# Hybrid layer, 8 batches on one core: the feed-forward residual enters the down product through VectorE, and the first and last batch are done in two parts

## The chip, the cores and the metric

The kernel runs on one core of one Trainium2 chip. Its time is the device time of one execution in microseconds (us); the median of several executions is compared.

## The reference, cut to what is computed

Each of 8 batches is a block `x` of 512 tokens x 128 channels in float32 and goes through five stages. `ln` is the plain normalization over channels with eps 1e-5.

```python
x = x + attention(ln(x))            # linear attention: ln(x) @ (Gram matrix of ln(x) @ Wq), no softmax
x = x + ffn(x)                      # f1
x = x + time_mix(ln(x))             # a recurrence over tokens with decay (maxima, exponentials), gate sigmoid(r), Wo
x = x + channel_mix(ln(x))          # square(relu(k)) @ Wv, gate sigmoid(r)
x = x + ffn(x)                      # f2

def ffn(x):
    y = ln(x)
    z = y + relu(y @ W1 + b1) @ W2 + b2      # 128 -> 512 -> 128
    return ln(z) * gamma + beta
```

The 16 feed-forwards (`f1` and `f2` of 8 batches) have the same weights. What matters here is the line of `z`: before its normalization, the down product needs `y + b2` added. Subtracting from each row of `z` its own mean changes nothing in `ln(z)`, so both kernels centre `W2` and `b2` over the channels.

## The kernel before, in words

A batch lies in SBUF as 128 partitions x 4 row blocks x 128 channels (`P` = 128, `J` = 4), in its own buffer `R[b]`, into which every stage adds. PSUM has 8 banks of 128 x 512; a call names its bank by number. Nothing schedules at run time: each engine has its order written out by hand as one long list of calls, such as `hidden_up(6, f2, 0, 2)` (batch, feed-forward, quarter, bank), and semaphores inside the calls make it wait. So the engine runs its list strictly in order, and a call that waits holds everything behind it. Batches overlap because the lists interleave calls of several batches.

One feed-forward `f` of batch `b` goes like this:

- VectorE `ffn_stats` and `mean_var` (L422, L460): statistics of `x`. GpSimd works out the scale (`shift`, `power`, `bias`), ScalarE writes `y` (`ffn_normed`, L758) into the ring `f1_y` or `f2_y`, which has 4 tiles.
- TensorE `ffn_transpose` (L993): 4 transposes of `y` into a bank. ScalarE `ffn_evacuate` (L813) copies them to `f_yT` and adds the centred `b2` (`B2C`) as bias.
- TensorE `hidden_up` (L1032): four products 128x512; each is evacuated by ScalarE `relu` (L821) into `f_h` with bias `B1C`. `B1C` is `b1` less what `B2C` brings into the up product, which TensorE `bias_part` (L1132) and VectorE `up_bias` work out at the start. The ring of `f_h` has 2 tiles.
- TensorE `ffn_start` (L1039): 4 transposes of `f_yT` against the identity, which put `y + b2` back into token order in the bank of the down product. This is done for 12 of the 16 feed-forwards. TensorE `ffn_down` (L1048): 4 quarters x 4 row blocks accumulate onto it.
- For the other 4 (`f2` of batches 1, 3, 5, 6, the table `IN_SBUF`) the down product starts at zero. GpSimd issues a DMA `down_residual` (L348) that adds `B2R` to `f_y` in SBUF, and VectorE `z_sum` (L449) adds the bank to it.
- VectorE `z_stats` (L422) or `z_sum_stats`, `mean_var`; GpSimd `z_shift` and `power` (L306, L311); VectorE `ffn_scaled` (L497) or `z_sum_scaled` (L508): 4 operations of 128x128; GpSimd issues the DMA `ffn_sum` that adds the result to `R[b]`. For `f1` of batch 0 and `f2` of batch 7 (`SPLIT`) VectorE does it itself instead: `ffn_gain` (L475) and `ffn_out` (L483).

The time mix has on VectorE the two recurrences `running_max` (L539) and `denominator_sum`/`numerator_sum`, and ends for each batch with VectorE `gated` (L598), TensorE `product_o` (L1078) and VectorE `tmix_out` (L606). The channel mix of that batch can start only then: its norm, TensorE `cmix_up` (L1090), `cmix_down` (L1096) and `gate_product` (L1107), then the norm and products of `f2`.

At the start the SP queue carries all loads, batches 0 and 1 first, and all weights. TensorE runs 24 transposes of the identity as warm-up, one small bias product, and 20 more transposes (`warm_up`, L1113) before the first Gram product (`attn_gram`, L1005). VectorE makes the normalized tile of batch 0 (`attn_normed`, L658) as a whole; `attn_out` (L466) adds attention to `R[b]`. `decay_along_tokens` clears `WROW` (L688) before it fills it. At the end the batch 7 result is made and stored as a whole.

The lines that carry this:

```python
IN_SBUF = {"f2": (1, 3, 5, 6)}
# ffn_start, TensorE
t_.matmul(banks[bank][:, j * C:(j + 1) * C], at(f.yT, b)[:, j * P:(j + 1) * P], IDENT[:], start=(j == 0), stop=False,
          is_transpose=True, skip_group_check=True)
# z_sum, VectorE
v.tensor_tensor(at(f.y, b)[:], bank_rows(bank), at(f.y, b)[:], ALU.add).then_inc(f.z_ready, 1)
```

## Time and profile before

| | us |
|---|---|
| median of 3 runs | 265.48 (265.29 to 265.97) |
| profiled execution | 266.14 |
| its span | 264.3 |
| granted TensorE clock, mean over the span | 0.992 |
| TensorE busy | 255.3 (97%) |
| VectorE busy | 228.2 (86%) |
| ScalarE busy | 227.2 (86%) |
| GpSimd busy | 159.0 (60%) |

The span runs from the first to the last instruction of the profiled execution; the 1.8 us that its time is longer lie around it. Busy time of an engine counts its records, and neighbouring records of one engine overlap a little, since an instruction is recorded until its last write while the next one is already in the pipeline. So the step from one start to the next tells what an operation costs in a row of them.

### The profile page before, as it was taken

What the parts mean: (1) busy time and instruction counts of PE and PEld (TensorE: products, weight loads), DVE (VectorE), ACT (ScalarE), POOL (GpSimd) and SP (SyncE); (2) the same over time, 40 slices, a digit from 0 to 9 for tenths busy, and PEclk for the clock granted to TensorE, in tenths of its full rate; (3) what the DMA queues carried; (4) which work ended last, traced back from release to release, by engine and by line L of the source; (5) the groups of instructions that cost most, each with busy time, mean ns of one, the idle gap of its engine ahead of it and who ended that gap; (6) DMA issues with size and microseconds to landing.
All of it is one profiled execution on the core that took longest, in us unless ns stands there. A gap on an engine that the chain in (4) does not pass through costs nothing. (4 is left out here: it accounts for less than half of the span.)

```text
span 264.3 us, 5318 instructions
## 1 busy us (share of the span) xinstructions
PE 255.3 (97%) x1544; PEld 191.7 (73%) x1544; DVE 228.2 (86%) x748; ACT 227.2 (86%) x440; POOL 159.0 (60%) x298
## 2 busy tenths in 40 slices
PE   7999999999999999999999999999999999999990
PEld 7987886866876686776588658757778658678770
DVE  3498569999999999999999999999999998637443
ACT  1397988999999999999989999999989979895630
POOL 4457676482498179179659827956069637445641
PEclk9999999999999999999999999999999999999996
DMA  6930420203022226303704130622046744725574
GB/s 184 297 110 0 82 42 1 42 15 64 2 42 40 40 42 103 58 2 67 133 2 75 18 67 2 119 41 43 0 71 120 126 85 115 126 43 87 118 150 122
DMA packets 18316, 19.15 MB, mean 72 GB/s; under 512 B 1520, under 2 KB 11632, under 8 KB 18288
## 3 DMA queue, kind: packets, MB, share of 16 engines
q0 software_dynamic: 7056, 12.85, 28.4%
q1 hardware_dynamic: 11232, 5.97, 8.0%
q8 instruction: 12, 0.20, 0.3%
q14 instruction: 16, 0.13, 0.2%
HBM read 3.87 MB, written 2.10 MB: 23 GB/s over the span
## 5 line engine op out<-in xcount | busy, mean ns | idle before, releaser
L1048 PEld LDWEIGHTS bank<-W,f_h 128*128 128x128 f32 x512 | 61.9, 192 | 8.4 <-issue 6.7
L1048 PE MATMUL bank<-W,f_h 128*128 128x128 f32 x512 | 64.3, 275 | 0.0
L1032 PE MATMUL bank<-f_yT,W 128*128 128x512 f32 x128 | 62.3, 598 | 0.0
L821 ACT ACTIVATE f_h<-bank,B1C 128x512 f32<-128x512 f32 x64 | 41.6, 681 | 9.5 <-PE bank L1032 8.2
L1096 PEld LDWEIGHTS bank<-FWv,KK 128*128 128x128 f32 x256 | 31.7, 192 | 5.0 <-issue 3.6
L1096 PE MATMUL bank<-FWv,KK 128*128 128x128 f32 x256 | 33.6, 275 | 0.0
L1032 PEld LDWEIGHTS bank<-f_yT,W 128*128 128x128 f32 x128 | 21.1, 190 | 16.7 <-issue 7.7
L1090 PE MATMUL bank<-XK,FWk 128*128 128x512 f32 x64 | 30.7, 599 | 0.0
L758 ACT ACTIVATE f_y<-R,f_yn_nb,f_yn_rs 128x128 f32<-128x128 f32 x64 | 26.3, 488 | 0.2 <-POOL f_yn_nb L315 0.2
L878 ACT ACTIVATE KK<-bank 128x512 f32<-128x512 f32 x32 | 18.4, 592 | 2.4 <-PE bank L1090 2.3
L882 ACT ACTIVATE KK<-KK 128x512 f32<-128x512 f32 x32 | 19.5, 625 | 0.1
L311 POOL TENSOR_TENSOR f_zn_rs<-f_zn_ve,K_RSQRT 128x4 f32<-128x4 f32 x16 | 18.9, 1183 | 0.5
L311 POOL TENSOR_TENSOR f_yn_rs<-f_yn_ve,K_RSQRT 128x4 f32<-128x4 f32 x16 | 18.6, 1161 | 0.0
L1090 PEld LDWEIGHTS bank<-XK,FWk 128*128 128x128 f32 x64 | 10.9, 190 | 9.8 <-issue 5.3
L339 POOL DMA_DIRECT2D R<-BETA x16 | 15.0, 964 | 4.6 <-ACT f_y L758 3.1
L293 POOL TENSOR_TENSOR tmix_tmp<-tmix_mv,K_EPS 128x4 f32<-128x4 f32 x8 | 2.5, 310 | 25.4 <-DVE tmix_mv L460 25.4
L306 POOL TENSOR_TENSOR f_zn_ve<-f_zn_mv,K_EPS 128x4 f32<-128x4 f32 x16 | 7.5, 469 | 16.6 <-DVE f_zn_mv L460 16.6
L364 POOL DMA_DIRECT2D R<-G x7 | 7.4, 1050 | 14.7 <-DVE G L634 14.7
L422 DVE BATCH_NORM_STATS2 f_yn_stats<-R 128x6 f32<-128x128 f32 x64 | 13.8, 278 | 2.0 <-DMA R<-G 1.7
L758 ACT ACTIVATE N<-R,tmix_nb,tmix_rs 128x128 f32<-128x128 f32 x32 | 13.1, 482 | 0.9 <-POOL tmix_nb L315 0.9
L758 ACT ACTIVATE NC<-N,cmix_nb,cmix_rs 128x128 f32<-128x128 f32 x32 | 13.1, 483 | 0.0
L284 POOL TENSOR_TENSOR f_yn_ve<-f_yn_mv,K_EPS 128x4 f32<-128x4 f32 x16 | 4.3, 270 | 14.5 <-DVE f_yn_mv L460 14.4
(144 smaller groups left out, 655.2 us busy)
## 6 DMA issues: line engine op xcount, KB each, us to landing
R<-BETA POOLq DMA_DIRECT2D x16, 256.0 KB, 3.4
R<-f_zg POOLq DMA_DIRECT2D x10, 256.0 KB, 3.4
R<-in_hidden SPq DMA_DIRECT2D x8, 256.0 KB, 3.9
R<-N POOLq DMA_DIRECT2D x8, 256.0 KB, 3.6
out_x<-R SPq DMA_DIRECT2D x8, 256.0 KB, 2.3
R<-G POOLq DMA_DIRECT2D x7, 256.0 KB, 3.5
f_y<-B2R POOLq DMA_DIRECT2D x4, 256.0 KB, 5.7
R<-f_y POOLq DMA_DIRECT2D x4, 256.0 KB, 3.9
```

The source lines that it names most:

```text
L306: pool.tensor_tensor(n.ve[b % 2][:], n.mv[b % 2][:, :, 1], K_EPS[:], ALU.add).then_inc(n.scale.sem(b), 1)
L311: pool.tensor_tensor(n.rs[b % 2][:], n.ve[b % 2][:], K_RSQRT[:], ALU.pow).then_inc(n.scale.sem(b), 1)
L339: pool.dma_start(R[b][:], BETA[:], accum_op=ALU.add).then_inc(*f.xb.step(b))
L422: last = v.bn_stats(n.stats[b % 2][:, j, :], src[:, j, :])
L758: done = a.activation(dst[:, j, :], src[:, j, :], ACT.Identity, scale=n.rs[b % 2][:, j:j + 1], bias=n.nb[b % 2][:, j:j + 1])
L821: a.activation(at(f.h, b)[:, n, :], banks[bank][:], ACT.Relu, bias=B1C[:, n:n + 1]).then_inc(f.h_ready[n], 1)
L878: a.activation(at(KK, b)[:, n, :], banks[bank][:], ACT.Relu).then_inc(square[n].sem(b), 1)
L882: a.activation(at(KK, b)[:, n, :], at(KK, b)[:, n, :], ACT.Square).then_inc(square[n].sem(b), 1)
L1032: t_.matmul(banks[bank][:], W1[:, n * P:(n + 1) * P], at(f.yT, b)[:], start=True, stop=True).then_inc(f.h_psum[n], 1)
L1048: last = t_.matmul(banks[bank][:, j * C:(j + 1) * C], at(f.h, b)[:, n, j * P:(j + 1) * P], W2[:, n, :], start=(n == 0 and j == 0 and b in ...
L1090: t_.matmul(banks[bank][:], FWk[:, n * P:(n + 1) * P], at(XK2, b)[:], start=True, stop=True).then_inc(kk_psum[n], 1)
L1096: last = t_.matmul(banks[bank][:, j * C:(j + 1) * C], at(KK, b)[:, n, j * P:(j + 1) * P], FWv[:, n, :], start=(n == 0 and j == 0), stop=(n ...
```

## The change

1. `ffn_start` moves from TensorE to VectorE. For all 16 feed-forwards VectorE writes `f_y + B2R` into the bank before the down products, with one `tensor_tensor` 128x512 (15 times), and for the last feed-forward with two, 128x384 and 128x128 (`last_start`). `ffn_down` always accumulates (`start=False`) and waits for that write (`f.y_psum`). The 48 transposes at L1039, `down_residual`, `z_sum`, `z_sum_stats` and `z_sum_scaled` are gone.
2. `ffn_evacuate` is a plain copy, `relu` takes `B1` as it is, and `bias_part` and `up_bias` are gone. `B2R` is one 128x128 tile, made by TensorE `bias_rows` (2 products) and VectorE `bias_rows_centred` (4 small operations).
3. The rings of `f_y` have 3 tiles instead of 4, those of `f_h` 1 instead of 2. `ffn_normed` waits for the VectorE write too before it overwrites a tile.
4. Batch 0: its load is two DMAs of 128 KB, and statistics, scale and `XN` are made in two halves of two row blocks (`first_stats`, `first_mean_var`, `first_shift`, `first_power`, `first_normed`).
5. Batch 7, `f2`: bias write, last down products, statistics, scale, gain, output and store are made in two parts, row blocks 0 to 2 and row block 3.
6. Loads: SP takes the 8 batches first, then the weights of the two mixes. The seven others (vectors, `Wq`, `W1`, `b1`, `W2`, `gamma`, `beta`) are issued by ScalarE's queue.
7. Warm-up: 10 float32 products of a zeroed tile, started as soon as VectorE has cleared it, and none after the bias products.
8. The lists of calls of all four engines are written anew, and with them the bank numbers.

The core of the diff:

```diff
-COPIES = {"N": 3, "f1_y": 4, "f2_y": 4, "f1_yT": 2, "f2_yT": 2, "f1_h": 2, "f2_h": 2, "XN": 3, "XNT": 2, "GRAM": 2,
-          "PROJ": 2, "f1_zg": 3, "f2_zg": 3, "others": 1}
+COPIES = {"N": 3, "f1_y": 3, "f2_y": 3, "f1_yT": 2, "f2_yT": 2, "XN": 3, "XNT": 2, "GRAM": 2, "PROJ": 2,
+          "f1_zg": 3, "f2_zg": 3, "others": 1}
-IN_SBUF = {"f2": (1, 3, 5, 6)}
+STARTED = {"f1": tuple(range(BATCHES)), "f2": tuple(range(BATCHES))}
+FIRST, LAST = ((0, 1), (2, 3)), ((0, 1, 2), (3,))
...
+            def ffn_start(b, f, bank, *free):
+
+                if b == f.started[0]:
+                    dve.wait_ge(*b2_rows.done(0, "centred"))
+                for s, count in free:
+                    dve.wait_ge(s, count)
+                dve.wait_ge(*f.norm.ready.done(b, "all"))
+                v.tensor_tensor(bank_rows(bank), at(f.y, b)[:], B2R[:].unsqueeze(1).broadcast_to([P, J, C]), ALU.add).then_inc(f.y_psum, 1)
...
             def ffn_down(b, f, n, bank, *free):
                 if b == 0:
-                    pe.wait_ge(w2_centred, 1)
-                freed(free)
+                    pe.wait_ge(*w2_rows.done(0, "centred"))
+                if b in f.started:
+                    pe.wait_ge(f.y_psum, f.started.index(b) + 1)
                 pe.wait_ge(f.h_ready[n], b + 1)
...
-                a.activation(at(f.yT, b)[:], banks[bank][:], ACT.Identity, bias=B2C[:]).then_inc(f.yT_ready, 1)
+                if b in f.started:
+                    a.activation(at(f.yT, b)[:], banks[bank][:], ACT.Copy).then_inc(f.yT_ready, 1)
...
+            def warm_up(bank, count):
+
+                pe.wait_ge(*warm.done(0, "tile"))
+                for _ in range(count):
+                    last = t_.matmul(banks[bank][:, 0:P], WROW[:, 0:P], WROW[:, 0:P], start=True, stop=True)
+                last.then_inc(warm.sem(0), 1)
```

How the lists move, at three places. A row is a line, an operation with its tiles, a shape and how many there are in a row.

**TensorE from the last `product_o` (batch 7) on.** Before, the first twelve rows from it (`L1048` is `ffn_down`, `L1032` `hidden_up`, `L1096` `cmix_down`, `L1090` `cmix_up`):

```order
L1078 MATMUL bank<-Wo,G 128x128 x4
L993 MATMUL bank<-IDENT,f_y 128x128 x4
L1048 MATMUL bank<-W,f_h 128x128 x8
L1032 MATMUL bank<-f_yT,W 128x512
L1096 MATMUL bank<-FWv,KK 128x128 x4
L1032 MATMUL bank<-f_yT,W 128x512
L1096 MATMUL bank<-FWv,KK 128x128 x4
L993 MATMUL bank<-IDENT,NC 128x128 x4
L1032 MATMUL bank<-f_yT,W 128x512
L1096 MATMUL bank<-FWv,KK 128x128 x4
L1032 MATMUL bank<-f_yT,W 128x512
L1090 MATMUL bank<-XK,FWk 128x512 x3
```

Now (`L1119` is `ffn_down`, `L1110` `hidden_up`, `L1187` `cmix_down`, `L1181` `cmix_up`, `L1198` `gate_product`):

```order
L1168 MATMUL bank<-Wo,G 128x128 x4
L1110 MATMUL bank<-f_yT,W 128x512 x3
L1187 MATMUL bank<-FWv,KK 128x128 x12
L1119 MATMUL bank<-W,f_h 128x128 x4
L1069 MATMUL bank<-IDENT,NC 128x128 x4
L1119 MATMUL bank<-W,f_h 128x128 x4
L1187 MATMUL bank<-FWv,KK 128x128 x4
L1119 MATMUL bank<-W,f_h 128x128 x4
L1181 MATMUL bank<-XK,FWk 128x512 x4
L1069 MATMUL bank<-IDENT,f_y 128x128 x4
L1119 MATMUL bank<-W,f_h 128x128 x4
L1198 MATMUL bank<-FWr,DC 128x128 x4
```

Three `hidden_up` products and the down products of channel mix 6 now stand together behind the last `product_o`, and down products of `f2` 4 and all those of `f2` 5 to 7. From the last `product_o` to the end of the list there were 16 products 128x512, 92 of 128x128 and 20 transposes; now there are 19, 104 and 16.

**VectorE before the first `running_max`.** Before (`L475` is `ffn_gain`, `L483` `ffn_out`, both of `f1` 0):

```order
L475 TENSOR_TENSOR f_zg<-bank,GAMMA 128x512
L422 BN_STATS f_zn_stats<-bank 128x6 x4
L422 BN_STATS attn_stats<-R 128x6 x4
L460 BN_AGGR f_zn_mv<-f_zn_stats 128x2 x4
L483 SCALAR_TENSOR_TENSOR R<-f_zg,f_zn_rs,R 128x128 x4
L422 BN_STATS tmix_stats<-R 128x6 x4
L460 BN_AGGR tmix_mv<-tmix_stats 128x2 x4
L466 TENSOR_TENSOR R<-bank,R 128x512
L422 BN_STATS f_yn_stats<-R 128x6 x4
L688 MEMSET WROW 128x512
L690 TENSOR_SCALAR WROW<-WROW,WDEC 128x512
```

Now (`L540`, `L548` are the same two, `L702` is `ffn_start`):

```order
L702 TENSOR_TENSOR bank<-f_y,B2R 128x512
L442 BN_STATS f_zn_stats<-bank 128x6 x4
L525 BN_AGGR f_zn_mv<-f_zn_stats 128x2 x4
L540 TENSOR_TENSOR f_zg<-bank,GAMMA 128x512
L702 TENSOR_TENSOR bank<-f_y,B2R 128x512
L548 SCALAR_TENSOR_TENSOR R<-f_zg,f_zn_rs,R 128x128 x4
L525 BN_AGGR attn_mv<-attn_stats 128x2 x4
L442 BN_STATS tmix_stats<-R 128x6 x4
L525 BN_AGGR tmix_mv<-tmix_stats 128x2 x4
L531 TENSOR_TENSOR R<-bank,R 128x512
L753 TENSOR_SCALAR WROW<-WROW,WDEC 128x512
```

`ffn_start` of `f1` 1 and 2 stand in front of and between the work on batch 0; the clearing of `WROW` is gone from here (it is the first call of the list). In all, 3 `ffn_start` stand ahead of the first `running_max`, and one `attn_out` and one `ffn_stats` with its `mean_var` fewer than before.

**VectorE around the last `gated` (`G<-EA,G`).** Before:

```order
L594 SCALAR_TENSOR_TENSOR G<-bank,G 128x512
L625 SCALAR_TENSOR_TENSOR DC<-DC,VEC,XC 128x512
L449 TENSOR_TENSOR f_y<-bank,f_y 128x512
L598 TENSOR_TENSOR G<-EA,G 128x512
L422 BN_STATS f_zn_stats<-f_y 128x6 x4
L460 BN_AGGR f_zn_mv<-f_zn_stats 128x2 x4
L606 SCALAR_TENSOR_TENSOR N<-N,tmix_back,bank 128x128 x4
L422 BN_STATS cmix_stats<-N 128x6 x4
L460 BN_AGGR cmix_mv<-cmix_stats 128x2 x4
L629 SCALAR_TENSOR_TENSOR G<-bank,G 128x512
L422 BN_STATS f_zn_stats<-bank 128x6 x4
```

Now:

```order
L688 TENSOR_TENSOR G<-bank,G 128x512
L648 SCALAR_TENSOR_TENSOR G<-bank,G 128x512
L652 TENSOR_TENSOR G<-EA,G 128x512
L442 BN_STATS f_zn_stats<-bank 128x6 x4
L660 SCALAR_TENSOR_TENSOR N<-N,tmix_back,bank 128x128 x4
L442 BN_STATS cmix_stats<-N 128x6 x4
L525 BN_AGGR cmix_mv<-cmix_stats 128x2 x4
L562 SCALAR_TENSOR_TENSOR f_zg<-bank,f_zn_rs,GAMMA 128x128 x4
L702 TENSOR_TENSOR bank<-f_y,B2R 128x512
L442 BN_STATS f_yn_stats<-R 128x6 x4
L525 BN_AGGR f_zn_mv<-f_zn_stats 128x2 x4
```

`z_sum` (`L449`) and its statistics are gone, and `ffn_start` of `f2` 4 stands behind `gated`. Between the first `running_max` and the last `gated` the list has now 9 `ffn_start` and one `attn_out` more, 2 `z_sum` and one scaling (4 operations of 128x128) fewer; nothing else changes in number there.

## Rows read from the trace of the kernel before

**Rows 1.** The page, first section: busy time, share of the span and instructions of each engine.
```profile
PE 255.3 (97%) x1544; PEld 191.7 (73%) x1544; DVE 228.2 (86%) x748; ACT 227.2 (86%) x440; POOL 159.0 (60%) x298
```

**Rows 2.** Busy time by stretch: us, busy (x) of PE, PEld, DVE, ACT, POOL; PEclk, DMA, GB/s.
```profile
9.50:45.60 36.10, 35.71 (x247) 28.96 (x246) 25.75 (x135) 30.79 (x77) 22.71 (x52) 1.00 0.32 75
45.60:220.10 174.50, 174.40 (x1019) 125.92 (x1017) 173.51 (x485) 168.73 (x313) 110.21 (x187) 1.00 0.31 55
220.10:257.60 37.50, 37.19 (x238) 28.82 (x237) 20.86 (x88) 26.43 (x51) 19.74 (x32) 1.00 0.56 104
```

**Rows 3.** Timeline of TensorE: start us, us, engine, line, operation, count.
```profile
253.55 3.73 PE L1048 MATMUL bank<-W,f_h 128*128 128x128 f32 x32
...
103.65 1.88 PE L1090 MATMUL bank<-XK,FWk 128*128 128x512 f32 x4
...
108.32 0.60 PE L993 MATMUL bank<-IDENT,f_y 128*128 128x128 f32 x4
```

**Rows 4.** Groups by line and shape: count | busy us, mean ns of one | idle before.
```profile
L1039 PE MATMUL bank<-IDENT,f_yT 128*128 128x128 f32 x48 | 7.2, 273 | 0.0
...
L449 DVE TENSOR_TENSOR f_y<-bank,f_y 128x512 f32<-128x512 f32 x4 | 2.7, 671 | 3.8 <-PE bank L1048 3.8
...
L688 DVE MEMSET WROW<- 128x512 f32 x1 | 0.5, 485 | 0.1
```

**Rows 5.** Timeline of VectorE: first `running_max`, last `gated`, last `tmix_out`.
```profile
45.57 1.22 DVE L539 TENSOR_TENSOR_SCAN PP<-WROW,bank 128x512 f32<-128x512 f32 x1
...
219.38 0.68 DVE L598 TENSOR_TENSOR G<-EA,G 128x512 f32<-128x512 f32 x1
...
221.38 1.12 DVE L606 SCALAR_TENSOR_TENSOR N<-N,tmix_back,bank 128x128 f32<-128x128 f32 x4
```

**Rows 6.** Timeline of TensorE, last `product_o`.
```profile
220.21 1.13 PE L1078 MATMUL bank<-Wo,G 128*128 128x128 f32 x8
```

**Rows 7.** Timeline of VectorE, two stretches of work back to back.
```profile
100.17 0.68 DVE L634 TENSOR_TENSOR G<-bank,G 128x512 f32<-128x512 f32 x1
100.77 0.68 DVE L614 TENSOR_TENSOR DC<-XC 128x512 f32<-128x512 f32 x1
...
203.44 1.13 DVE L508 SCALAR_TENSOR_TENSOR f_y<-f_y,f_zn_rs,GAMMA 128x128 f32<-128x128 f32 x4
204.49 0.86 DVE L422 BATCH_NORM_STATS2 cmix_stats<-N 128x6 f32<-128x128 f32 x4
```

**Rows 8.** Timeline of VectorE, the start.
```profile
3.54 0.87 DVE L422 BATCH_NORM_STATS2 attn_stats<-R 128x6 f32<-128x128 f32 x4 [3.54 <-DMA R<-in_hidden]
...
6.43 1.11 DVE L658 TENSOR_SCALAR XN<-R,attn_mv,attn_rs 128x128 f32<-128x128 f32 x4 [0.43 <-POOL attn_rs L311]
...
13.30 0.69 DVE L466 TENSOR_TENSOR R<-bank,R 128x512 f32<-128x512 f32 x1 [3.33 <-PE bank L1020]
...
33.98 1.14 DVE L483 SCALAR_TENSOR_TENSOR R<-f_zg,f_zn_rs,R 128x128 f32<-128x128 f32 x4 [1.42 <-POOL f_zn_rs L311]
```

**Rows 9.** Timeline of TensorE, the start: warm-up, first Gram product, last down products of `f1`, batch 0.
```profile
1.53 5.38 PE L1113 MATMUL bank<-IDENT 128*128 128x128 f32 x24 [1.53 <-POOL IDENT L264]
...
7.00 2.67 PE L1113 MATMUL bank<-IDENT 128*128 128x128 f32 x20
...
9.50 1.06 PE L1005 MATMUL bank<-XN 128*128 128x128 f32 x8
...
27.96 1.95 PE L1048 MATMUL bank<-W,f_h 128*128 128x128 f32 x16
```

**Rows 10.** Timelines of VectorE and GpSimd, the end.
```profile
257.32 0.89 DVE L422 BATCH_NORM_STATS2 f_zn_stats<-bank 128x6 f32<-128x128 f32 x4 [2.78 <-PE bank L1048]
...
258.98 1.03 POOL L311 TENSOR_TENSOR f_zn_rs<-f_zn_ve,K_RSQRT 128x4 f32<-128x4 f32 x1
...
260.05 1.14 DVE L483 SCALAR_TENSOR_TENSOR R<-f_zg,f_zn_rs,R 128x128 f32<-128x128 f32 x4 [0.85 <-POOL f_zn_rs L311]
```

**Rows 11.** The page, last section: line engine op xcount, KB, us to landing.
```profile
out_x<-R SPq DMA_DIRECT2D x8, 256.0 KB, 2.3
```

798 lines of the change are left out of this document (424 added, 374 removed).

## The prediction, made before the changed kernel was run

> **What bounds the kernel now.** I read the page's busy shares first [rows 1]: TensorE is 97% busy and VectorE 86%. Such a mean hides stages, so next comes the busy time by stretch [rows 2], cut at the first `running_max`, at the last `gated` and at TensorE's last product [rows 5]. The reader is to see three regimes. In 45.6 to 220.1 TensorE has records over all of it, but VectorE too: 173.51 of 174.50 us. A matmul's record includes waiting in a full pipeline, so I count TensorE's work instead. The steps are 0.427 us for a pass of 512 columns ((1.88 - 0.6) / 3), 0.1115 us for one of 128 ((3.73 - 0.275) / 31), 0.108 us for a transpose ((0.60 - 0.275) / 3) [rows 3]; a float32 product has two passes. By these the whole list is 242.4 us before. From the last `product_o`, at 220.21 [rows 6], the listed 32 long passes (13.7), 184 short ones (20.5) and 20 transposes (2.2) are 36.4 us, and the trace takes 37.1 up to TensorE's end at 257.3. So the last stretch is bounded by TensorE, which works off what it has left over, while VectorE is busy 20.86 of 37.5 us there. The middle is bounded by VectorE: its list between the two landmarks is 175.9 us by such steps, and the trace took 174.5. In the first stretch VectorE is busy 25.75 of 36.1 us: it waits there in turn for TensorE, GpSimd and DMAs [rows 8, 9]. So there are four terms: start of the middle, its length on VectorE, the rest on TensorE, and the end.
>
> My landmarks are the start of the first `running_max` (45.57), the last `gated`, the last product, and the end of the span (264.3).
>
> **The start: -5.3 us.** Batch 0's statistics begin at 3.54, when 256 KB have landed; TensorE's first Gram product is held until 9.50 by the second warm-up block, 2.67 us from 7.00, although `XN` is there from 7.5 on [rows 8, 9]. Now the first half needs 128 KB, and no warm-up stands behind the bias products. I walked the new lists with the old durations. First statistics at 3.1 (estimate: 0.4 less for half the load), `XN` whole at 6.9, `attn_out(0)` at 10.85 instead of 13.30, so 2.45 less. The first up product comes at 17.8. The last down product of `f1` 0 ended at 29.9 (27.96 + 1.95) and ends at 25.8: the four start transposes and two products that stood in front are gone. From there `ffn_out(0)`, time-mix norm, transposes, `mix_k` and `product_k` follow as before. Had they kept their distance, `running_max(0)` would come 4.1 us earlier; VectorE's list ahead of it has 3 starts more (+1.8) and one `attn_out` and one norm pass less (-1.7), so it is about 30 us either way and doesn't hold it. Some of the 16 us of idle time that remain are filled by the new order. I take 40.3, thus -5.3. Ends: -3.5 (only the changes at batch 0, with a wait at the moved loads) and -12 (VectorE never idle after 3.1: 3.1 + 30.2 = 33.3).
>
> The new warm-up is a question of its own. The first 24 transposes took 5.38 us, twice the step of the later 20, although the profile shows a granted clock of 1.00 there [rows 9]. If the products from 7 us on ran at that double step, some 3 us of it would be on the path; this is in the low end of the -3.5.
>
> **The middle, VectorE: +3.7 us.** Between `running_max(0)` and `gated(7)` come in 9 `ffn_start` and one `attn_out`; 2 `z_sum` go, and one scaling of four 128x128. A start is a `tensor_tensor` 128x512 from SBUF into PSUM with a broadcast operand. No row before has it. The nearest rows are adds that read a bank, step 100.77 - 100.17 = 0.60 us [rows 7], with a record of 671 ns [rows 4]; the lowest is the clearing of 128x512 at 485 ns [rows 4], the highest the four 128x128 at 1.05 [rows 7]. I take 0.60, nearest in shape and operands; the ends 0.45 and 0.75 make +-1.4. So 9 x 0.60 + 0.60 - 2 x 0.60 - 1.05 = +3.75. In this stretch every start counts in full, since VectorE is idle for under 1 us of it. The time TensorE saves here is not on the path: 9 of the 12 x 4 transposes it loses, and only 146 to 164 us of listed work in 158 to 178 us. ScalarE's list between its gate calls is 158 us before and 159 after. It saves 16 x 0.09 us on the copies without bias, and isn't the one that is late. I cost both at nothing. `down_residual` goes from GpSimd, four issues of some 2 us each, on an engine that is 60% busy [rows 1]: nothing. The shorter rings cost nothing either: `ffn_normed(b)` needs the reading of `y` of batch b-3, and `relu` of b the downs of b-1, which stand ahead of its up products at nearly all places. If that cover fails, the price is in the slower case below.
>
> **After the last `product_o`, TensorE: +4.8 us.** The order excerpt shows what moved. Behind it stand now 38 long passes (16.2), 208 short (23.2) and 16 transposes (1.7), together 41.2 us against 36.4. The 48 transposes at L1039 are 5.2 us of TensorE's list [rows 3, 4], yet only four of them stood here. The new order has TensorE idle in the middle and leaves it 19 products instead of 16 for the end. VectorE isn't in the way there: 20.86 us before plus some 5 in 41. Ends: +3 (part of these products is done while `tmix_out(7)` and its norm would leave TensorE waiting anyway; but the row shows only 0.7 us of such waits now) and +6.
>
> By the Trainium skill, "Perfetto Trace Analysis", Identifying the Most-Contended Engine, matmul busy time is no good measure for TensorE, and the busy share of weight loads is to be read in its place. That is 73% over the span [rows 1] and 28.82 of 37.5 us, 77%, in this stretch [rows 2]. By that rule TensorE isn't the bound here, and this term would fall away; the sum by rows says 36.4 of 37.1.
>
> **The end: -0.9 us.** From the last product to the end are 7.06 us: statistics at 257.32, power 1.03 us at 258.98, `ffn_out` 260.05 to 261.19 [rows 10], then the store, 256 KB in 2.3 us from issue to landing [rows 11]. Now three quarters of it start two products (0.45 us) before the last. Powers follow each other on GpSimd, so the second ends at about +2.9 and the last `ffn_out` at +3.5 instead of +3.9; 64 KB land sooner, by 0.5 as an estimate (nothing to 1.1). Ends: -0.3 and -1.6.
>
> **Sum.** -5.3 + 3.7 + 4.8 - 0.9 = +2.3 us. The profiled execution takes 266.14 with a span of 264.3, so it would be 268.4. It stands 0.66 above the median of 265.48, so the median is forecast at **267.8**. A difference of 0.3% (0.8 us) is what a measurement of this kernel can tell from none.
>
> **The rivals.**
>
> *A, faster: the start gains more.* 16 us of idle time stand in VectorE's first stretch, and the new lists put starts, statistics and the later batches' attention between the waits. If `running_max(0)` comes at 35.3, 5 us sooner than in my walk and 2 above the floor, the time is 262.8. For: the order was changed most here, and seven loads left the SP queue. Against: the chain of `f1` 0 (transposes, up, relu, down, norm, power) is no shorter by its own links.
>
> *B, the skill's rule.* TensorE isn't the bound of the last stretch, and the added products fill gaps: 267.8 - 4.8 = 263.0. Against: the 36.4 of 37.1 above.
>
> *C, the same.* A start gain of 7.5 us: -7.5 + 3.7 + 4.8 - 0.9 = +0.1, 265.5.
>
> *D, slower: a start holds VectorE.* `ffn_start` waits in VectorE's strict order for ScalarE's `y` and, in 9 calls, for a bank to be read by another engine. Behind it stand the operations of the recurrence, which nothing else feeds. With the forecast otherwise, 12 such starts at 0.3 us each put on 3.3 to 3.6 us: 271. It decides from 0.1 us per start on. For: the old lists had no such wait, and VectorE has no slack. Against: they were placed where the bank should have been free.
>
> That the change doesn't do what it says is out: the list has no transposes against `f_yT` any more, and 15 + 2 writes on VectorE.
>
> **How the numbers follow.** Forecast 0.42 (267.8), A 0.28 (262.8), C 0.17 (265.5), D 0.10 (271), B 0.03 (263.0). Faster takes A and B, 0.31; same is C, 0.17; slower is the forecast and D, 0.52. The forecast's own range is 265.8 to 269.8. The range for 8 in 10 is 262.5 to 271.0: it takes in A's and D's middle and leaves out their far halves.
>
> **What would show it.** `running_max(0)` near 40.3; from there to the last `gated` about 178 us with VectorE idle for under 2; TensorE from the last `product_o` to its end about 41.9; from there to the end 6.2; `ffn_start` at 0.60 per step with no wait for banks. The prediction is wrong if `running_max(0)` is before 37, if TensorE's idle time in the middle is small so that the products of the end move forward, or if VectorE's starts show idle time ahead of them.

## The result, and the profile after

The changed kernel takes 272.94 us (median of 4, 270.95 to 273.63) against 265.73 us for the kernel before, run beside it. The ratio is 1.0252, 95% interval 1.0184 to 1.032: it is slower by 2.5%. The forecast was 267.8 us with a range up to 271.0. The direction was right, the size was not: +2.3 us were forecast, +7.2 us came.

The profiled execution of the changed kernel is its fastest, 270.95 us with a span of 269.2, 4.9 us above that of the kernel before. The other 2 us of the median are differences between executions; the traces of the experiments show two such differences. An execution over 1.5% longer than the fastest of its kernel counts in the medians and ranges below but in no ratio (one of a_res, the profiled one; two of a_chain; one of the kernel before, of 939 us).

The page's first section, then the busy time by stretch, cut at the same landmarks as in [rows 2] (columns as there):

```profile
PE 249.8 (93%) x1464; PEld 184.5 (69%) x1464; DVE 235.0 (87%) x764; ACT 227.3 (84%) x439; POOL 159.1 (59%) x296
```

```profile
42.30:220.80 178.50, 171.22 (x973) 121.45 (x971) 176.53 (x489) 167.96 (x312) 110.21 (x182) 1.00 0.27 46
220.80:262.40 41.60, 41.60 (x263) 32.12 (x262) 24.23 (x103) 29.94 (x58) 21.60 (x36) 1.00 0.56 105
262.40:269.20 6.80, 0.04 (x1) 0.00 (x0) 2.70 (x13) 0.00 (x0) 1.78 (x4) 0.77 0.68 158
```

In the middle VectorE is busy nearly all the time as before, while TensorE now has gaps: 171.22 of 178.50 us busy, where it had none in [rows 2]. Behind the last `product_o` TensorE has no gap in 41.6 us. The landmarks themselves, from the timelines of VectorE and TensorE (first `running_max`; last `gated`; last `product_o`; start of the last block of products; first statistics of the end), which answer to [rows 5, 6, 10]:

```profile
42.33 1.21 DVE L593 TENSOR_TENSOR_SCAN PP<-WROW,bank 128x512 f32<-128x512 f32 x1
...
220.00 0.69 DVE L652 TENSOR_TENSOR G<-EA,G 128x512 f32<-128x512 f32 x1 [0.70 <-ACT G L946]
```

```profile
220.88 1.09 PE L1168 MATMUL bank<-Wo,G 128*128 128x128 f32 x8
...
260.49 1.95 PE L1139 MATMUL bank<-W,f_h 128*128 128x128 f32 x16
```

```profile
262.03 0.69 DVE L447 BATCH_NORM_STATS2 f_zn_stats<-bank 128x6 f32<-128x128 f32 x3 [2.69 <-PE bank L1139]
```

The terms of the prediction, in us of the two profiled executions:

| term | before | after | measured | forecast |
|---|---|---|---|---|
| start of `running_max(0)` | 45.57 | 42.33 | -3.2 | -5.3 |
| from there to the start of the last `gated` | 173.8 | 177.7 | +3.9 | +3.7 |
| from there to the last `product_o` | 0.8 | 0.9 | 0 | 0 |
| from there to TensorE's end | 37.1 | 41.6 | +4.5 | +4.8 |
| from there to the end of the span | 7.0 | 6.8 | -0.3 | -0.9 |
| sum | 264.3 | 269.2 | +4.9 | +2.3 |

The two large losses have about the forecast size. The two gains are too small, and the timed executions lose more still. So I looked at the start first. VectorE's timeline:

```profile
3.16 0.49 DVE L447 BATCH_NORM_STATS2 attn_stats<-R 128x6 f32<-128x128 f32 x2 [1.76 <-DMA R<-in_hidden]
...
6.83 0.87 DVE L442 BATCH_NORM_STATS2 attn_stats<-R 128x6 f32<-128x128 f32 x4 [2.13 <-DMA R<-in_hidden]
7.62 0.58 DVE L467 TENSOR_SCALAR XN<-R,attn_mv,attn_rs 128x128 f32<-128x128 f32 x2
8.12 0.28 DVE L719 TENSOR_SCALAR DIAG<-IDENT,VEC 128x128 f32<-128x128 f32 x1
8.32 0.59 DVE L467 TENSOR_SCALAR XN<-R,attn_mv,attn_rs 128x128 f32<-128x128 f32 x2
...
13.80 0.69 DVE L531 TENSOR_TENSOR R<-bank,R 128x512 f32<-128x512 f32 x1 [0.32 <-PE bank L1097]
```

The first half of batch 0 is there at 3.16, as thought. But VectorE's list has the statistics of batch 1 ahead of `first_normed(0)`. They wait 2.13 us for their load, until 6.83, and XN(0), which needs nothing of batch 1, stands behind them. In the kernel before the statistics of batch 1 began at 4.75, behind those of batch 0, and XN(0) at 6.43 [rows 8]. TensorE in the same stretch, and the granted clock by windows (PEclk is the third column from the end, 1.00 is 2.4 GHz):

```profile
1.46 4.63 PE L1206 MATMUL bank<-WROW 128*128 128x128 f32 x20 [1.46 <-DVE WROW L713]
8.55 0.46 PE L1213 MATMUL bank<-DIAG,MEAN 128*128 128x128 f32 x2 [2.46 <-DVE DIAG L719]
...
8.98 1.14 PE L1082 MATMUL bank<-XN 128*128 128x128 f32 x8
9.96 1.01 PE L1069 MATMUL bank<-IDENT,XN 128*128 128x128 f32 x4
...
11.92 1.85 PE L1097 MATMUL bank<-PROJ,XNT 128*128 128x128 f32 x8 [0.52 <-ACT PROJ L873]
13.60 0.60 PE L1069 MATMUL bank<-IDENT,XN 128*128 128x128 f32 x4
```

```profile
9.00:10.00 1.00, 1.00 (x12) 1.00 (x11) 0.96 (x8) 0.00 (x0) 0.72 (x3) 1.00 1.08 328
10.00:11.00 1.00, 1.00 (x8) 1.00 (x5) 0.55 (x3) 0.28 (x1) 0.79 (x2) 0.51 1.20 301
11.00:12.00 1.00, 0.48 (x3) 0.22 (x2) 1.00 (x12) 0.99 (x3) 0.32 (x3) 0.50 1.22 290
12.00:14.00 2.00, 2.00 (x12) 2.00 (x13) 1.61 (x9) 2.00 (x6) 1.53 (x5) 0.64 1.16 297
```

The warm-up ends at 6.1, and TensorE has nothing to do for 2.46 us. It starts again with a step of 0.12 us in the first Gram product, and from 10 to 13 us it runs at the lower of its two levels, 0.50 of the clock: four transposes take 1.01 us where they take 0.60 later, eight passes of `attn_apply` 1.85 instead of 1.13. At the end, `last_out` waits 0.90 us for a DMA, R<-BETA:

```profile
264.96 1.14 DVE L493 SCALAR_TENSOR_TENSOR R<-f_zg,f_zn_rs,R 128x128 f32<-128x128 f32 x4 [0.90 <-DMA R<-BETA]
```

### The profile page after: what moved, and what is told of

It is laid out like the page before. It is cut to its first block and busy times, and to the rows that moved or that the text cites. A ratio compares the mean times of both kernels' runs of the same rounds, so it can differ in the third digit from the quotient of the medians.

```text
span 269.2 us, 5220 instructions
## 1 busy us (share of the span) xinstructions
PE 249.8 (93%) x1464; PEld 184.5 (69%) x1464; DVE 235.0 (87%) x764; ACT 227.3 (84%) x439; POOL 159.1 (59%) x296
## 5 line engine op out<-in xcount | busy, mean ns | idle before, releaser
L1119 PEld LDWEIGHTS bank<-W,f_h 128*128 128x128 f32 x480 | 58.1, 192 | 9.1 <-issue 9.1
L1110 PE MATMUL bank<-f_yT,W 128*128 128x512 f32 x128 | 62.1, 595 | 1.1 <-ACT f_yT L881 0.8
L1119 PE MATMUL bank<-W,f_h 128*128 128x128 f32 x480 | 61.3, 276 | 1.1 <-ACT f_h L895 0.9
L895 ACT ACTIVATE f_h<-bank,B 128x512 f32<-128x512 f32 x64 | 41.8, 685 | 8.3 <-PE bank L1110 5.7
L1187 PEld LDWEIGHTS bank<-FWv,KK 128*128 128x128 f32 x256 | 31.6, 192 | 7.7 <-issue 5.0
L1187 PE MATMUL bank<-FWv,KK 128*128 128x128 f32 x256 | 32.9, 276 | 0.0
L1110 PEld LDWEIGHTS bank<-f_yT,W 128*128 128x128 f32 x128 | 21.7, 191 | 15.5 <-issue 12.7
L1181 PE MATMUL bank<-XK,FWk 128*128 128x512 f32 x64 | 31.0, 597 | 0.5 <-ACT f_yT L881 0.3
L288 POOL TENSOR_TENSOR f_yn_ve<-f_yn_mv,K_EPS 128x4 f32<-128x4 f32 x16 | 7.3, 455 | 35.5 <-DVE f_yn_mv L525 35.4
L377 POOL DMA_DIRECT2D R<-f_zg x14 | 14.1, 1009 | 9.3 <-DVE f_zg L562 8.8
L1181 PEld LDWEIGHTS bank<-XK,FWk 128*128 128x128 f32 x64 | 11.0, 190 | 10.8 <-issue 7.5
L562 DVE SCALAR_TENSOR_TENSOR f_zg<-bank,f_zn_rs,GAMMA 128x128 f32<-128x128 f32 x56 | 15.6, 340 | 2.9 <-issue 2.9
L336 POOL TENSOR_TENSOR f_zn_ve<-f_zn_mv,K_EPS 128x4 f32<-128x4 f32 x15 | 5.6, 375 | 19.7 <-DVE f_zn_mv L525 19.6
L341 POOL TENSOR_TENSOR f_zn_rs<-f_zn_ve,K_RSQRT 128x4 f32<-128x4 f32 x15 | 16.2, 1080 | 0.9
L442 DVE BATCH_NORM_STATS2 f_zn_stats<-bank 128x6 f32<-128x128 f32 x60 | 13.2, 282 | 2.7 <-PE bank L1119 2.7
L702 DVE TENSOR_TENSOR bank<-f_y,B2R 128x512 f32<-128x512 f32 x15 | 10.3, 690 | 4.2 <-ACT f_y L828 4.1
```

Source lines behind the costliest of these rows:

```text
L341: pool.tensor_tensor(n.rs[b % 2][:], n.ve[b % 2][:], K_RSQRT[:], ALU.pow).then_inc(n.scale.sem(b), 1)
L377: pool.dma_start(R[b][:], at(tile, b)[:], accum_op=ALU.add).then_inc(*f.out.step(b))
L562: last = v.scalar_tensor_tensor(zg[:, j, :], z[:, j, :], f.znorm.rs[b % 2][:, j:j + 1], GAMMA[:], ALU.mult, ALU.mult)
L895: a.activation(at(f.h, b)[:, n, :], banks[bank][:], ACT.Relu, bias=bias[:, n:n + 1]).then_inc(f.h_ready[n], 1)
L1110: t_.matmul(banks[bank][:], W1[:, n * P:(n + 1) * P], at(f.yT, b)[:], start=True, stop=True).then_inc(f.h_psum[n], 1)
L1119: last = t_.matmul(banks[bank][:, j * C:(j + 1) * C], at(f.h, b)[:, n, j * P:(j + 1) * P], W2[:, n, :], start=False, stop=(n == H - 1), sk ...
```

## The experiments

All times are medians; "before" ran beside each group, with medians of 265.6 to 266.5 us and single executions from 264.7 to 267.6. The landmarks are those of each run's profiled execution: the first Gram product, the start of `running_max(0)`, the middle from there to the start of the last `gated`, the rest from the last `product_o` to TensorE's end. The edits are on the changed kernel, except the `b_` runs, which are on the kernel before.

| run | median (range) | Gram | running_max(0) | middle | rest |
|---|---|---|---|---|---|
| before | 265.5 | 9.50 | 45.57 | 173.8 | 37.1 |
| changed | 272.94 (270.95 to 273.63) | 8.98 | 42.33 | 177.7 | 41.6 |
| a_order | 273.31 (272.56 to 274.60) | 7.06 | 42.97 | 179.4 | 41.6 |
| a_warm | 272.67 (271.96 to 273.72) | 8.84 | 41.10 | 180.5 | 41.6 |
| a_oneq | 273.00 (272.36 to 273.37) | 6.83 | 41.45 | 180.5 | 41.6 |
| a_res | 275.29 (273.39 to 278.48) | 9.41 | 44.59 | 181.6 | 43.0 |
| a_warm_break | 270.60 (269.76 to 271.83) | 9.12 | 41.78 | 178.2 | 42.4 |
| a_start | 270.89 (270.17 to 271.18) | 7.45 | 40.78 | 178.4 | 41.6 |
| a_start_break | 270.01 (269.84 to 270.33) | 6.88 | 41.15 | 178.2 | 41.6 |
| a_nostart | 271.34 (270.62 to 272.00) | 8.86 | 44.15 | 176.6 | 41.5 |
| a_pestart | 274.37 (273.66 to 276.54) | 8.77 | 42.81 | 178.6 | 43.3 |
| sb_nostart | 267.95 (267.04 to 269.12) | 7.05 | 41.82 | 176.3 | 41.5 |
| sb_pestart | 272.01 (271.83 to 272.76) | 6.84 | 41.92 | 177.5 | 43.3 |
| a_lessdown | 271.88 (270.62 to 274.12) | 8.41 | 41.75 | 179.4 | 41.2 |
| a_chain | 275.63 (271.37 to 276.11) | 8.74 | 44.11 | 179.4 | 42.3 |
| a_chain_less | 271.61 (269.99 to 273.89) | 9.49 | 44.97 | 179.4 | 40.1 |
| b_dummy | 269.90 (269.66 to 270.48) | 8.56 | 45.10 | 177.8 | 37.1 |
| b_warm | 264.47 (264.27 to 264.68) | 7.79 | 43.95 | 173.8 | 37.1 |
| b_first | 264.30 (263.71 to 265.31) | 7.45 | 44.10 | 173.8 | 37.1 |
| b_best | 263.85 (263.76 to 264.52) | 6.47 | 43.22 | 173.8 | 37.1 |

### The start

**a_order.** XN(0) ahead of the statistics of batch 1.

```diff
-            first_normed(0); bias_diagonal(); first_normed(1); mean_var(1, na); attn_stats(2)
+            first_normed(0); bias_diagonal(); first_normed(1); attn_stats(1); mean_var(1, na); attn_stats(2)
```

(`attn_stats(1)` stood at the end of the line ahead of these.)

> Edit, on the changed kernel: VectorE makes XN of batch 0 (first_normed of both halves) before it takes the statistics of batch 1, not behind them. Theory 1 (VectorE's strict order: XN(0) stands behind the load of batch 1, so TensorE is idle from 6.09 to 8.55 us and then runs its next work at the low clock until 13): XN(0) is whole at about 6.7 instead of 8.9, the first Gram product comes at about 6.9 instead of 8.98, the recorded clock stays at 1.00, running_max(0) comes 2 to 3.5 us earlier than 42.33, and the kernel is 2 to 5 us faster than the changed one (272.94), 268 to 271. Rival (the later chain of the first feed-forward sets the start, not XN(0)): running_max(0) moves by less than 0.7 us, and the time stays within 1 us.

The first Gram product came at 7.06, as expected, but `running_max(0)` at 42.97 and the time at 273.31: no gain. TensorE's timeline of this run shows where the 1.9 us went:

```profile
9.66 1.13 PE L1097 MATMUL bank<-PROJ,XNT 128*128 128x128 f32 x8 [0.47 <-ACT PROJ L873]
13.22 0.66 PE L1069 MATMUL bank<-IDENT,XN 128*128 128x128 f32 x4 [2.43 <-DVE B2C L729]
13.71 1.59 PE L1082 MATMUL bank<-XN 128*128 128x128 f32 x8
15.10 1.06 PE L1069 MATMUL bank<-IDENT,XN 128*128 128x128 f32 x4
```

The transposes of batch 1 wait 2.43 us for B2C, since they go into bank 7, which holds the bias rows until B2C has been made from them. VectorE does that in `bias_rows_centred`, and this call stands in its list behind the statistics of batches 2, 3 and 4, which wait for their loads. After the pause TensorE soon runs at half rate again (1.06 us for four transposes; granted clock 0.50 from 15 to 17 us). The wait was already in the changed kernel's list, covered by the late XN(0).

**a_warm.** A longer warm-up.

```diff
-            warm_up(0, 10)
+            warm_up(0, 18)
```

> Edit, on the changed kernel: 18 warm-up products instead of 10, so that TensorE has no pause between 6.09 and 8.55 us. Nothing else changes. Theory of the clock (the fall to 0.5 of the clock from about 10 to 13 us follows the pause, and is worth over 1 us, more in the executions of 273.6 us): the clock stays at 1.00 there, the first Gram product is at most 0.5 us later, attn_out(0) comes at about 12.3 instead of 13.8, the median falls by 1 to 3 us and the executions of one kernel lie closer together than 270.95 to 273.63. Rival (the slow stretch is hidden behind GpSimd and ScalarE): no change beyond 0.7 us.

The clock stayed at 1.00, `attn_out(0)` came at 12.57 instead of 13.80 and `running_max(0)` at 41.10 instead of 42.33: the half clock was worth 1.2 us of the start in the profiled execution. Yet the time hardly moved (272.67). The middle had become 2.9 us longer, which is taken up below.

**a_oneq.** All loads on the SP queue, in the old order.

```diff
             load_x0(1)
+            sp.dma_start(Wq[:], w_q).then_inc(first_loaded, DMA)
+            sp.dma_start(VEC[:], vectors).then_inc(first_loaded, DMA)
             load_x0(2)
...
-            act.dma_start(VEC[:], vectors).then_inc(first_loaded, DMA)
-            act.dma_start(Wq[:], w_q).then_inc(first_loaded, DMA)
...
```

> Edit, on the changed kernel: all loads on the SP queue in the order of the kernel before, the first batch still in two halves; nothing is loaded by ScalarE's queue. Theory (two queues side by side share the 16 DMA engines, so batch 1, which XN(0) waits for in VectorE's order, lands at 6.8 us instead of about 5): its statistics start at about 5.0 to 5.4, XN(0) is whole 1.5 us earlier, the time falls by 1 to 3 us. Rival (batch 1 is late only by its place behind another load, or Wq and the vectors then come later on the one queue and hold the Gram and projection products): the start stays within 0.7 us or gets later.

Batch 1's statistics began at 4.67, the Gram product at 6.83; then the same kind of wait for B2C, 2.57 us, this time with no fall of the clock behind it, and the same longer middle as in a_warm: 273.00. So with the second queue batch 1 came 2 us later. `running_max(0)` came 0.9 us earlier than in the changed kernel, and the end gained nothing.

**a_start.** As a_order, and `bias_rows_centred` moved up, with 12 warm-up products.

```diff
-            mean_var(2, na); mean_var(3, na); attn_stats(4); bias_rows_centred(); attn_out(0, 0); ffn_stats(0, f1)
+            mean_var(2, na); mean_var(3, na); attn_stats(4); attn_out(0, 0); ffn_stats(0, f1)
...
+            first_normed(1); attn_stats(1); mean_var(1, na); bias_rows_centred(); attn_stats(2); attn_stats(3)
...
-            warm_up(0, 10)
+            warm_up(0, 12)
```

> Edit, on the changed kernel: on VectorE XN of batch 0 is made ahead of the statistics of batch 1, and bias_rows_centred ahead of the statistics of batch 2 (in the runs a_order and a_oneq TensorE stood idle for 2.4 us at attn_transpose(1), which waits for it, and bias_rows_centred stood behind the loads of batches 2 and 3); 12 warm-up products instead of 10. Theory (each gain at batch 0 was lost to the next VectorE call that stood behind a load, and TensorE's half clock followed each pause): the first Gram product at about 7.2, no pause of TensorE over 1 us before 18 us and no step of 0.21 us behind the warm-up, running_max(0) at 39.5 to 41, so 1.3 to 2.8 us before that of the changed kernel. Rival (something later in the start, the norm chain of f1 0 or its loads, holds): running_max(0) at 41.5 or later. What the time does depends on the middle: 269 to 272.

`running_max(0)` came at 40.78, where the prediction had 40.3, and the four executions lie within 1.01 us: 270.17 to 271.18. The walk of the prediction isn't confirmed by that, though: `attn_out(0)` came at 12.20, not 10.85, and the 1.35 us were made up for on the way to `running_max(0)`. The median fell by 2 us, though the middle (178.4) is no better than in the trace of the changed kernel. What timed executions of the changed kernel may have lost at the start can be seen in other runs that share it. In a_res, a_nostart, a_chain and a_chain_less `running_max(0)` came at 44.1 to 45.0, not 42.3. TensorE's timeline of a_res:

```profile
9.41 2.06 PE L1082 MATMUL bank<-XN 128*128 128x128 f32 x8
11.26 1.06 PE L1069 MATMUL bank<-IDENT,XN 128*128 128x128 f32 x4
...
13.27 2.04 PE L1097 MATMUL bank<-PROJ,XNT 128*128 128x128 f32 x8 [0.52 <-ACT PROJ L873]
...
15.96 1.78 PE L1082 MATMUL bank<-XN 128*128 128x128 f32 x8
17.58 0.60 PE L1069 MATMUL bank<-IDENT,XN 128*128 128x128 f32 x4
```

There the fast step (0.60 us for four transposes) comes only at 17.58; everything before it takes twice as long, although the windows give a granted clock of 1.00 there (a_nostart and a_chain read the same; a_chain_less reads 0.50 from 9 to 18 us). With the same start in the lists, TensorE is at either level from one trace to the next. What it goes with is the pause: in all seven traces that share this start (the changed kernel, a_res, a_lessdown, a_nostart, a_pestart, a_chain, a_chain_less) 1.8 to 3.0 us pass between the 10 warm-up products and the next work, and each then runs at half rate for 3 to 9 us. In the eight other traces of the new order the pause is 1.5 us or less, and the first Gram product and its transposes run at the fast step.

### The middle

In a_warm and a_oneq the middle was 180.5 us instead of 177.7, with an edit that ended at 14 us. VectorE's idle time had grown around 127 us, in front of `gate_log(3)`, which waits for ScalarE, which waits for GpSimd's `bias(2, ncm)` (cmix_nb). GpSimd's timeline of a_warm, and VectorE's of the same microseconds:

```profile
119.67 1.03 POOL L341 TENSOR_TENSOR cmix_rs<-cmix_ve,K_RSQRT 128x4 f32<-128x4 f32 x1
120.78 1.78 POOL L345 TENSOR_TENSOR cmix_nb<-cmix_nm,cmix_rs 128x4 f32<-128x4 f32 x1
```

```profile
120.63 0.73 DVE L569 TENSOR_TENSOR DX<-XA 128x512 f32<-128x512 f32 x1
121.23 1.27 DVE L638 TENSOR_TENSOR EA<-AB,EA 128x1024 f32<-128x1024 f32 x1
...
127.11 0.69 DVE L648 SCALAR_TENSOR_TENSOR G<-bank,G 128x512 f32<-128x512 f32 x1 [1.11 <-ACT G L942]
```

An operation of 128x4, which takes 0.20 us elsewhere, took 1.78 us there, and 3.7 us in a_res (below). (a_res was profiled in its longest execution, 278.48 us.) While it waits VectorE runs operations with two tensors in SBUF, back to back. In a_warm it ends as the second of them does, in a_res as VectorE turns to statistics:

```profile
124.27 3.71 POOL L345 TENSOR_TENSOR cmix_nb<-cmix_nm,cmix_rs 128x4 f32<-128x4 f32 x1
```

```profile
124.11 0.74 DVE L569 TENSOR_TENSOR DX<-XA 128x512 f32<-128x512 f32 x1
124.71 1.28 DVE L638 TENSOR_TENSOR EA<-AB,EA 128x1024 f32<-128x1024 f32 x1
125.84 0.81 DVE L581 SCALAR_TENSOR_TENSOR XV<-DX,VEC,XA 128x512 f32<-128x512 f32 x1
126.51 0.75 DVE L644 SCALAR_TENSOR_TENSOR G<-G,EA 128x512 f32<-128x512 f32 x1
127.11 0.81 DVE L575 SCALAR_TENSOR_TENSOR XK<-DX,VEC,XA 128x512 f32<-128x512 f32 x1
127.77 0.95 DVE L442 BATCH_NORM_STATS2 f_zn_stats<-bank 128x6 f32<-128x128 f32 x4
```

The Trainium skill, "SBUF — State Buffer", Who interferes with whom, says that a VectorE instruction with two SBUF inputs and a GpSimd instruction that reads SBUF contend for a shared port, and that whoever issues first holds it for the whole instruction. The rows agree that the two keep each other out, but the wait outlasts one instruction: two of them in a_warm, five in a_res (124.27 to 127.98), where it ends with the first one that reads one tensor.

**a_warm_break.** One call moved, on top of a_warm, so that the run of such operations has a gap.

```diff
-            tmix_change(4); with_current(3); mix_v(4); gate_sum(3); mix_k(4); z_stats(6, f1, 6)
-            tmix_stats(5); gate_log(3, 1)
+            tmix_change(4); tmix_stats(5); with_current(3); mix_v(4); gate_sum(3); mix_k(4); z_stats(6, f1, 6)
+            gate_log(3, 1)
```

> Edit, on the run with 18 warm-up products: VectorE takes tmix_stats(5), four statistics with one tensor input each, between tmix_change(4) and with_current(3), where there was a run of five operations with two tensors in SBUF each; before, it stood behind that run. Theory P (in that run GpSimd's small operation bias(2, ncm) cannot start, 1.58 us with the longer warm-up and 3.5 us in the run with the earlier residual, and from it ScalarE's channel-mix norm, gate and VectorE's gate_log are late; that makes the middle 180.5 us instead of 177.7): bias(2, ncm) takes under 1.2 us, VectorE's idle time at gate_log(3) is under 0.7 instead of 1.11, the middle from running_max(0) to the last gated is 177.5 to 179.5, and the time falls by 1 to 3 us from 272.67. Rival (the middle's extra 2.9 us are elsewhere, the idle time at gate_log(3) is set by TensorE or the DMAs): the middle stays at 180 to 181.

`bias(2, ncm)` took 0.64 us, the idle time at `gate_log(3)` went, the middle fell from 180.5 to 178.2 and the time by 2.1 us to 270.60. So theory P holds for the wait, but not for the whole of the 2.9 us that it set out to explain. The time from `running_max(3)` to `running_max(5)` tells them apart:

| traces | `bias(2, ncm)` | from `running_max(3)` to `(5)` |
|---|---|---|
| changed | 0.20 | 46.7 |
| a_warm_break, a_start_break | 0.64 | 47.3 |
| a_order, a_start, a_lessdown, a_chain, a_chain_less | 1.78 | 48.4 to 48.5 |
| a_warm, a_oneq | 1.78 | 49.6 |
| a_res | 3.71 | 50.6 |

The wait of 1.78 us is worth 1.1 to 1.2 us against the broken run of operations and 1.7 us against the trace of the changed kernel. The further 1.1 us of a_warm and a_oneq go with TensorE's clock. In a_start and in a_warm alike TensorE stands idle for 1.65 us and 0.51 us around this place, since ScalarE is late; then the two passes of the product behind `mix_k` take 1.13 us in a_start and 1.70 in a_warm, where the window reads a clock of 0.50 (third column from the end; 0.53 in a_res from 130 to 132 us). In a_warm `running_max(4)` then waits 0.55 us for that product, in a_start not at all. Why the clock fell in one and not in the other isn't shown. The rows of a_start, of a_warm, and the window of a_warm:

```profile
125.32 1.13 PE L1152 MATMUL bank<-XK,Wk 128*128 128x512 f32 x2 [0.51 <-ACT f_h L895]
```

```profile
126.61 1.70 PE L1152 MATMUL bank<-XK,Wk 128*128 128x512 f32 x2 [0.51 <-ACT f_h L895]
```

```profile
128.00:130.00 2.00, 2.00 (x10) 1.90 (x9) 1.66 (x2) 2.00 (x5) 0.00 (x0) 0.50 0.04 12
```

Whether GpSimd's operation waits seems to hang on a tenth of a microsecond. In the trace of the changed kernel it starts 0.06 us before VectorE's `tmix_change` (DX), where it waits it starts 0.02 to 0.16 us behind it. Why it gets through after two operations in most traces and after five in a_res isn't shown. It waits in all ten other traces of the new order in which the run of operations isn't broken, so the changed kernel's profiled execution, its fastest, is the lucky one.

**a_start_break.** Both together.

> Edit: as a_start, and tmix_stats(5) between tmix_change(4) and with_current(3) as in a_warm_break. Theory (start and the locked-out GpSimd operation are separate and add up): running_max(0) as in a_start, bias(2, ncm) under 1 us, middle 177.5 to 178.5, time 267.5 to 269.5, near the forecast of 267.8. Rival (GpSimd's luck only moves to another of its operations): middle 179.5 or more.

270.01 us, 269.84 to 270.33: somewhat above what I expected. The middle was within it, `running_max(0)` came 0.4 us later than in a_start. This is the changed kernel without these accidents, and it is still 1.6% slower than before (1.0117 to 1.0202). Its terms are -4.4, +4.4, +4.5 and -0.3 us, +4.2 in all where +2.3 were forecast. Against a_start the break gave 0.9 us of the time.

**a_nostart, a_pestart; sb_nostart, sb_pestart.** The write of `y + b2` cut to one column (`[:, 0, 0:1]` of bank, `f_y` and `B2R`), without and with TensorE's transposes in its place; `sb_` on top of a_start_break. They leave `y + b2`, or `b2`, out of `z`.

```diff
-                v.tensor_tensor(bank_rows(bank), at(f.y, b)[:], B2R[:].unsqueeze(1).broadcast_to([P, J, C]), ALU.add).then_inc(f.y_psum, 1)
+                v.tensor_tensor(bank_rows(bank)[:, 0, 0:1], at(f.y, b)[:, 0, 0:1], B2R[:, 0:1], ALU.add).then_inc(f.y_psum, 1)
```

> Edit, on the changed kernel: each of the 17 writes of y + b2 is one column of 128x1 instead of 128x512, in the same place and with the same waits, and the down product starts at zero; y + b2 is left out of z. It takes 0.5 us each off VectorE and nothing off any other engine. Theory (VectorE bounds the middle, so each of its starts counts in full there; TensorE the rest): the 9 starts of the middle give 4 to 5 us, from 177.7 to about 173, the end from the last product_o stays at 41 to 41.6, and the time falls by 4 to 7 us to about 267.5 (with the three starts ahead of running_max(0)). Rival (GpSimd's and ScalarE's chains or TensorE bound the middle, and VectorE's added work is hidden): under 2 us.

> Edit, on the changed kernel: as the run with one column, and besides TensorE puts y into the bank by 4 transposes of f_yT ahead of the first down product, as the kernel before did, for all 16 feed-forwards; b2 is left out. So the new order of calls with the start on TensorE. 64 transposes are 6.9 us of TensorE work, 16 of them behind the last product_o. Theory (the middle is VectorE's, with room on TensorE; behind the last product_o all is TensorE's): middle about 1 us above the run with one column, the end from product_o 1.7 us longer, 43.3; in all 2 to 3 us slower than with one column, 269 to 271. Rival (TensorE is the bound of the middle too once it has the transposes back): middle 3 us or more above it, as slow as the changed kernel or slower.

The first pair was blurred by its starts (44.15 and 42.81). But the middle did not fall to 173 with 4.5 us of VectorE's work gone: 176.6, with 4.4 us idle. The clean pair:

> Edit: a_pestart on top of a_start_break, so without the bad start: the 17 writes of y + b2 are one column each, and TensorE puts y into the bank by 16 x 4 transposes; b2 is left out. This is the new order with its start mended and the start of the down product as in the kernel before. Theory (VectorE's 9 writes bound the middle, TensorE's transposes cost only in the rest): middle 174 to 177 instead of 178.2, rest 43.3 instead of 41.6, so the time within 1.5 us of a_start_break's 270.0, 268.5 to 271. Rival (TensorE bounds the middle as well once it has the transposes): middle over 178.5, time over 272.

> Edit: a_nostart on top of a_start_break: the new order with its start mended, the 17 writes of y + b2 one column each, no transposes; y + b2 is left out. Against a_start_break (270.0) it gives what the write costs on VectorE in the new order, against sb_pestart (272.0) what the transposes cost on TensorE. Theory (a stand-in of 0.6 us counted 0.57 us each in the old order, so VectorE's full price would be 4.5 us in the middle; but sb_pestart, with the 9 writes gone, had its middle only 0.75 us shorter, with 4.7 us of idle time on VectorE, so in the new order other waits take the write's place): middle 175.5 to 177, rest 41.5, time 267.5 to 269.5. Rival (sb_pestart's middle was held by the transposes, and without them the 4.5 us come off): middle under 174.5.

Against a_start_break (270.01) the 17 writes together are worth 2.1 us of the time (267.95), 1.9 of it in the middle. The transposes in their place are worth 4.1 (272.01); of that the profiled executions show 1.7 in the rest and 1.1 in the middle. So in the new order VectorE is the better place for the start. But even with no start at all the new order is slower than the kernel before (1.0077, 1.0045 to 1.0108), and that kernel has 12 starts and 4 sums in its time.

**b_dummy.** One more operation of 128x512 on VectorE ahead of each `tmix_change`, in the old order.

```diff
             def tmix_change(b):
+                v.tensor_tensor(SCRATCH[:], BETA[:], GAMMA[:].unsqueeze(1).broadcast_to([P, J, C]), ALU.add)
```

> Edit, on the kernel before: one more tensor_tensor of 128x512 on VectorE ahead of each tmix_change, that adds gamma to beta into a tile nobody reads; 7 of the 8 lie between running_max(0) and the last gated. Nothing waits for it and TensorE has the same work. Theory (VectorE bounds the middle, each 0.60 us operation counts in full): middle 173.8 + 4.2 = 178.0, time 269 to 270.5. Rival (half or more of it is hidden under waits of the other engines): middle under 176.

The middle went from 173.8 to 177.8: 4.0 us for 7 operations, 0.57 each. In the old order such an operation counts nearly in full. The time rose by 1.4% (1.0101 to 1.0176).

### Behind the last product_o, and the end

**a_lessdown.** Quarters 1 and 2 of the down products of `f2` 5 and 6 for one row block instead of four. The others are left out of the result.

```diff
-                for j in range(J):
+                for j in range(1 if f is f2 and b in (5, 6) and n in (1, 2) else J):
```

> Edit, on the changed kernel: in the second feed-forwards of batches 5 and 6 the quarters 1 and 2 of the down product are made for one row block instead of four; 12 products of 128x128 are left out, 24 passes of 0.1115 us or 2.7 us of TensorE, all behind the last product_o. Theory (TensorE's rest bounds the stretch of 41.6 us behind product_o): that stretch falls to 38.8 to 39.2, nothing ahead of it moves, and 2.5 us go from the time. Rival (it is bound by VectorE, ScalarE and GpSimd in turn, with TensorE's records only filled by waiting): it falls by under 1 us.

The rest fell by 0.4 us only, 41.6 to 41.2, with 2.7 us less of TensorE's work. By itself this says that TensorE doesn't bound it. The timeline shows another limit: the chain of batch 7 (TensorE now waits 0.73 us for ScalarE's last `f_y`). In the kernel before its last `cmix_down` began 20.1 us behind `product_o`, now 24.2 us, since four other calls stand ahead of it in TensorE's list:

```profile
241.09 1.05 PE L1187 MATMUL bank<-FWv,KK 128*128 128x128 f32 x8
241.98 1.95 PE L1119 MATMUL bank<-W,f_h 128*128 128x128 f32 x16
243.77 1.02 PE L1110 MATMUL bank<-f_yT,W 128*128 128x512 f32 x2
244.63 0.60 PE L1069 MATMUL bank<-IDENT,f_y 128*128 128x128 f32 x4
245.06 1.06 PE L1187 MATMUL bank<-FWv,KK 128*128 128x128 f32 x8
```

From there the chain goes on through `cmix_gated`, the norm of `f2` 7 and ScalarE's `f_y`, which ends 32.7 us behind `product_o`; TensorE comes to its transposes at 33.0. The two limits lie 0.3 us apart.

**a_chain, a_chain_less.** `cmix_down(7, 3)` right behind `cmix_down(7, 2)`, and the calls of ScalarE and VectorE that follow from it moved up (TensorE's list shown); then the same with the products left out.

```diff
-            hidden_up(5, f2, 1, 0, (f2.zg_ready, 5)); cmix_down(7, 2, 6); ffn_down(5, f2, 0, 7); ffn_down(5, f2, 1, 7)
-            hidden_up(5, f2, 2, 0); ffn_transpose(6, f2, 2); cmix_down(7, 3, 6); ffn_down(5, f2, 2, 7)
+            hidden_up(5, f2, 1, 0, (f2.zg_ready, 5)); cmix_down(7, 2, 6); cmix_down(7, 3, 6); ffn_down(5, f2, 0, 7); ffn_down(5, f2, 1, 7)
+            hidden_up(5, f2, 2, 0); ffn_transpose(6, f2, 2); ffn_down(5, f2, 2, 7)
```

> Edit, on the changed kernel, behind the last product_o: TensorE makes cmix_down(7, 3) right behind cmix_down(7, 2) and not 4 us later; ScalarE's cgate_back(7) stands ahead of ffn_normed(6) and ffn_normed(7) ahead of the relus of batch 6; VectorE's cmix_gated(7), cmix_out(7) and ffn_stats(7) ahead of ffn_start(6). So batch 7's y is ready some 3 us sooner; TensorE's work is the same. Two limits are held to lie within 0.5 us of each other there: TensorE's own 41.2 us of work, and the chain of batch 7 through channel mix and norm. If both are real: the stretch from product_o to TensorE's end stays at 41.0 to 41.6. If only the chain bounds it (rival, since 2.7 us less of TensorE's work gave 0.4): 38.5 to 40.

> Edit: a_chain and a_lessdown together (chain of batch 7 sooner, and 2.7 us of down products of batches 5 and 6 left out). If both limits are real: the stretch is now 38.5 to 39.2, over 2 us less than with either edit alone. If only the chain bounds it: as a_chain. If a third thing does (the last feed-forward's own ups, relus and downs behind a later wait): over 40.5.

With `f_y(7)` done 3.9 us sooner, at 28.8, the rest was 42.3, not shorter but 0.7 longer: TensorE stands idle for 0.48 us ahead of the last down products of `f2` 5. In a_chain_less, with the same wait, the profile puts it down to ScalarE's `f_h`, and the edit had put a call of ScalarE ahead of these `relu`. With the products left out as well it was 40.1, 2.2 us less than a_chain for 2.7 us of work; I had expected 38.5 to 39.2. Only with both edits does the rest fall clearly below the 41.6 of the changed kernel, by 1.5 us. So both limits are real, and they lie close together. (Both traces have the bad start, so their times say nothing.)

**a_res.** The last `ffn_residual` moved up in GpSimd's list.

```diff
-            z_shift(5, f2); power(5, f2.znorm)
+            ffn_residual(7, f2); z_shift(5, f2); power(5, f2.znorm)
...
-            ffn_sum(6, f2, f2.zg); ffn_residual(7, f2); last_shift(0)
+            ffn_sum(6, f2, f2.zg); last_shift(0)
```

> Edit, on the changed kernel: the last ffn_residual (DMA that adds beta to batch 7) is issued in GpSimd's list before the scale of batch 5's second feed-forward and not as the last DMA. Theory (the two-part end gained 0.3 us instead of 0.9 because last_out waits for that DMA, which is issued at 260.18 and lands at about 264.9): last_out starts at about 264.2 after last products at 262.4, and 0.7 us go from the end. Rival (the end is set by the second part's own power and store): nothing changes by over 0.3 us.

`last_out` no longer waited for the DMA and began 2.4 us behind `last_stats(0)` instead of 2.9, but from those statistics to the end of the span are 7.1 us as in the changed kernel (7.2), and 7.0 before. The rival holds: without the wait for the DMA the end is as long, with the second part's own power (0.55 us, until 272.69) and a store of 64 KB that lands in 1.9 us where 256 KB took 2.3 [rows 11]. The time itself, 275.29, goes with three losses in its trace. The half-step start and the locked-out operation are far from the edit. The third is the edit's own: the moved call waits 2.07 us for `f_y` of batch 7, and the scale of `f2` 5 now stands behind it in GpSimd's list; TensorE in the end waits 1.12 us for `ffn_scaled`, and the rest is 43.0.

### The start by itself, in the old order

**b_warm.** A shorter second warm-up block.

```diff
-            warm_up(0, 24); centre_bias(); warm_up(0, 20); attn_gram(0, 0)
+            warm_up(0, 24); centre_bias(); warm_up(0, 6); attn_gram(0, 0)
```

> Edit, on the kernel before: the second warm-up block has 6 transposes instead of 20. XN(0) is ready there at 7.5 us and the first Gram product stands behind the block at 9.50. Theory (the start carries through to the end, since the middle has no slack on VectorE): first Gram product at about 7.8, attn_out(0) 1.5 us earlier, running_max(0) 0.5 to 1.7 us earlier, time 264 to 265, the clock at 1.00. Rivals: the loads of batches 2 and 3 or the later chain hold and nothing moves (265.2 to 265.9); or the shorter block lets the clock fall and the time rises over 266.

**b_first.** Part 4 of the change put into the kernel before: two half loads, `first_stats` to `first_normed`, XN(0) ahead of `attn_stats(1)`, 4 transposes behind the bias product. Two groups of semaphores were merged to make room. One hunk of several:

```diff
-            attn_stats(0); mean_var(0, na); attn_stats(1); mean_var(1, na); attn_normed(0); centre_down_bias()
+            first_stats(0); first_mean_var(0); first_stats(1); first_mean_var(1); first_normed(0); first_normed(1); centre_down_bias(); attn_stats(1); mean_var(1, na)
```

> Edit, on the kernel before: part 4 of the change by itself, batch 0 loaded and normalized in two halves, with XN(0) ahead of the statistics of batch 1, and 4 transposes instead of 20 in the second warm-up block. Everything else, the starts on TensorE and all other calls in their places, is as before. Theory: XN(0) at about 6.3 and the first Gram product at about 7.3, running_max(0) at 43 to 44.5 instead of 45.57, middle, rest and end as before, time 263 to 264.8: a version faster than both. Rival (the gain at batch 0 is lost to the next call that waits for a load, as in a_order): running_max(0) within 0.5 us of before, time 265 to 266.

**b_best.** On b_first:

```diff
-            warm_up(0, 24); centre_bias(); warm_up(0, 4)
+            warm_up(0, 21); centre_bias(); warm_up(0, 3)
...
-            bias_part(); attn_apply(0, 0)
+            attn_apply(0, 0); bias_part()
```

> Edit, on b_first: 21 and 3 warm-up transposes instead of 24 and 4, and bias_part behind attn_apply(0) and not ahead of it (TensorE waited 0.44 us there for W1). Theory: the first Gram product at 6.7 to 7.0 instead of 7.45, attn_out(0) about 1 us earlier, running_max(0) at 43.3 to 43.8, time 263.2 to 264.0. Rival (the clock falls or rises later with less warm-up, or a later wait takes the gain): 264.3 or more.

264.47, 264.30 and 263.85: all three beat both kernels (intervals from 0.990 to 0.996), b_best by 0.6% of the kernel before (ratio 0.9939, 0.9916 to 0.9962). The gain at `running_max(0)` (1.6, 1.5, 2.4 us) arrives at the end nearly whole, with middle, rest and end unchanged. Up to 0.5 us of it is chance: b_dummy, whose start is untouched, has its `running_max(0)` at 45.10. The halves by themselves gave next to nothing over the shorter warm-up: in b_first XN(0) was whole at 6.4 and the Gram product was still held by the warm-up and the bias product until 7.45. For b_best a clean start came with it:

```profile
1.53 3.96 PE L1161 MATMUL bank<-IDENT 128*128 128x128 f32 x21 [1.53 <-POOL IDENT L271]
5.89 0.35 PE L1167 MATMUL bank<-VEC,MEAN 128*128 128x1 f32 x2 [0.41 <-DMA VEC<-in_vectors]
6.11 0.53 PE L1161 MATMUL bank<-IDENT 128*128 128x128 f32 x3
6.47 1.11 PE L1053 MATMUL bank<-XN 128*128 128x128 f32 x8
```

## Why the prediction was wrong

- **The start, -5.3 us, is the step that failed.** "`XN` whole at 6.9, `attn_out(0)` at 10.85": I walked the list with the old durations and took batch 1 to be there when its statistics were due. It landed at 6.8, XN(0) stood behind it in VectorE's list and was whole at 8.9, and `attn_out(0)` came at 13.80, no earlier than before. The excess over the forecast was 2.1 us in the profiled execution. With the order mended (a_start), `running_max(0)` came at 40.78, within 0.5 us of the walk; that is in part luck, since `attn_out(0)` was at 12.20 even then.
- **The warm-up.** I had priced the double step at up to 3 us of the low end and then taken none of it. It costs 1.2 us in the profiled execution (a_warm) and about 2 us more where the fast step comes only at 17 us. The traces with this loss are those with a pause of 1.8 us or more behind the warm-up; in b_warm, with 0.5 us between a shorter warm-up and the first Gram product, nothing is lost.
- **The middle, +3.7 us, came out as +3.9**, but its mechanism was half right. "Every start counts in full" holds in the old order (b_dummy, 0.57 us each). In the new one the writes are worth 1.9 us, and the other 2.5 us of the middle are there without them (sb_nostart, 176.3 against 173.8). VectorE is idle for 4.1 us of that middle, and for 1.0 before; which part of the new order makes these waits was not tried and stays open. That the sum of the list fitted is therefore in part luck. (The prediction also set its list of 175.9 us against 174.5, which is the time up to `product_o`; up to the last `gated` it is 173.8, so the list counts 2 us more than the trace took.) What it lacked altogether is GpSimd's locked-out operation: 1.7 us over the trace of the changed kernel where it waits 1.78 us, 2.9 where TensorE's clock falls behind it. The timed executions left no trace, so in how many of them it waited stays open; in the ten other traces without the break it always did. Rival D named a VectorE start held by a bank or by `y` as the slower case; no such idle time shows in front of the 9 starts of the middle.
- **The rest, +4.8 us, came out as +4.5.** It is TensorE's work, and beside it, 0.3 us away, the later channel mix of batch 7, which I hadn't seen. Rival B (263.0) missed: the weight loads are 32.12 of 41.60 us, 77% again, and the stretch grew with the products. The prediction had also misread the rule that it set against the sum. The Trainium skill, "Perfetto Trace Analysis", Identifying the Most-Contended Engine, names the engine with the highest share, with achieved rate and weight loads standing for TensorE's. By weight loads TensorE had 77% of the stretch before, ScalarE 70% (26.43 of 37.5) and VectorE 56%, so the rule too points at TensorE. What the 77% doesn't show is how little room was left: 36.4 of 37.1 us by the sum of steps.
- **The end, -0.9 us, gave -0.3.** From the last statistics to the end are 7.2 us instead of 7.0, even with the DMA out of the way 7.1: the two parts gained nothing there. The 0.3 us are the two products by which these statistics start sooner.
- **Rivals A and C** needed a larger gain at the start. The best start of any run on the new order is 40.78, far from A's 35.3.
- **The range** was made around one profiled execution. The upper end of 271.0 held a mishap of 3 us, but not two at once. The profiled execution of 270.95 lies within it, the median doesn't: the further 2 us are differences between executions, for which the late start (1.8 to 2.6 us) and the locked-out operation (1.7 us or more) are the candidates that other traces show.

## What to carry to other kernels

When a call moves ahead of another in an in-order list, ask what it waits for, and who stands behind it without needing it: a statistic of batch 1 held the tile of batch 0, and behind that a bias row stood behind the loads of batches 2 to 4. When TensorE's warm-up is shortened, end it where the first real product begins: here 1.8 to 3.0 us of pause behind it went with half rate for 3 to 9 us, though not every later pause of that length did (2.57 us in a_oneq). And an order that is good in one execution can be 2 us worse in the next: look at the spread of the runs, and compare the same stretch in several traces, before trusting a sum made from one profile.

## What the hardware showed that I had not expected

- GpSimd's 128x4 operation of 0.20 us took 1.8 to 3.7 us while VectorE ran operations with two SBUF tensors back to back; one call of statistics between them was worth 0.9 us (a_start_break) to 2.1 us (a_warm_break) of the kernel. The larger figure holds a second loss: TensorE waited for what hung on it, and its clock fell to 0.50 for some 3 us.
- TensorE ran at double step (0.25 us per pass of 128 where 0.12 is usual in these rows) from 9.4 to 17.5 us in some executions of the same start while the granted clock of the windows read 1.00; in a_chain_less, with the same steps, it read 0.50. Early in a span the step between records tells the level here, that column doesn't always.
- Cutting 2.7 us of TensorE's work from a stretch without a gap on TensorE gave 0.4 us: records back to back don't show that a second limit lies just under the first.
